# Attention and mixture of experts on one core: a row's expert numbers and shares written by GpSimd, low parts in halves, a new item order

## The reference

```python
x = _layernorm(x + attention(x))      # 16 heads of 16, 4 key/value heads, causal
x = _layernorm(x + ffn(x))
# attention: q, k, v projections, rotation by head number, softmax(q k^T / 4) v, output projection
# ffn:
scores = sigmoid(gate_w x) + gate_b                 # 16 experts
weights, indices = top_k(scores, 4)
weights = weights / weights.sum(-1)
shared = silu(x @ w1_shared) * (x @ w3_shared) @ w2_shared
routed = sum over the 4 experts of weight * (silu((x @ w1[e]) * (x @ w3[e])) @ w2[e])
out = shared + routed
```

## Time and profile before

| | us |
|---|---|
| median of 3 runs | 535.52 (535.23 to 536.46) |
| the profiled execution's own time | 534.25 |
| its span, first to last instruction | 532.5 |
| TensorE busy | 506.3 |
| VectorE busy | 435.0 |
| ScalarE busy | 373.2 |
| GpSimd busy | 292.0 |
| chain that ended last: TensorE, VectorE, ScalarE, GpSimd | 63%, 22%, 6%, 5% |

### The profile page before, as it was taken

One profiled execution on the slowest core, in us unless ns is written; L12 is line 12 of the kernel. 1 busy time (PEld: TensorE's weight loads), 2 busy tenths in 40 slices (PEclk: granted clock), 3 DMA queues, 4 the chain that ended last, 5 costly groups with the idle time before them and its releaser, 6 DMA issues.

```text
span 532.5 us, 12191 instructions
## 1 busy us (share of the span) xinstructions
PE 506.3 (95%) x3775; PEld 359.0 (67%) x3775; DVE 435.0 (82%) x1102; ACT 373.2 (70%) x845; POOL 292.0 (55%) x340
## 2 busy tenths in 40 slices
PE   8789999999999999899999997999999999999895
PEld 5545554545454646355432696899999999999884
DVE  3699998899999999989971479978878877877685
ACT  3527878788988978769889573466766766667444
POOL 5404354454315677777778592777555445445292
PEclk9989999999999999999999999999999999999998
DMA  5464350074034893201422631577543433331595
GB/s 154 94 164 62 78 86 19 3 160 84 1 95 121 182 215 94 82 33 50 130 77 81 183 92 41 181 244 232 154 135 129 121 119 114 117 115 45 192 414 186
DMA packets 53182, 64.96 MB, mean 122 GB/s; under 512 B 8139, under 2 KB 46686, under 8 KB 53120
## 3 DMA queue, kind: packets, MB, share of 16 engines
q1 hardware_dynamic: 45072, 45.60, 32.0%
q0 software_dynamic: 7344, 18.38, 10.1%
q10 hardware_dynamic: 704, 0.20, 0.2%
HBM read 32.49 MB, written 25.62 MB: 109 GB/s over the span
## 4 chain that ended last, share of the span: by engine, by line
PE 63%; DVE 22%; ACT 6%; POOL 5%; issue 3%; DMA 1%; DVEq 0%; ACTq 0%; POOLq 0%
PE psH L1820 15%; DVE MX L1265 10%; PE psO L1602 8%; PE psS L1617 8%; PE psT L1587 7%; PE psX L1788 3%; PE psG L1831 3%; PE psS L1684 2%; ACT prob L953 2%; PE psY L1844 2%; PE psY L1848 2%; PE psY L1845 2%; PE psY L1847 2%; PE psY L1846 2%; PE psS L1622 2%
## 5 line engine op out<-in xcount | busy, mean ns | idle before, releaser
L953 ACT ACTIVATE prob<-psT 128x512 f32<-128x512 f32 (+3 forms) x384 | 166.0, 497 | 34.1 <-PE psT L1587 31.3
L1265 DVE TENSOR_REDUCE MX<-psS 128x1 f32<-128x512 f32 (+3 forms) x304 | 178.9, 652 | 5.0 <-PE psS L1622 2.0
L1617 PE MATMUL psS<-KS,QS 96*128 96x512 bf16 (+3 forms) x384 | 108.0, 330 | 5.2 <-DVE MX L1265 2.8
L906 POOL DMA_INDIRECT y_scratch<-ys,dst x79 | 77.0, 974 | 65.6 <-ACT ys L1115 50.6
L1587 PE MATMUL psT<-QS,KS 98*128 98x512 bf16 (+3 forms) x384 | 107.2, 328 | 0.4
L829 POOL DMA_INDIRECT xs_scratch<-x1row,slotu x64 | 64.8, 1012 | 30.4 <-issue 15.3
L1820 PE MATMUL psH<-wU,xh 128*128 (+1 forms) x380 | 80.9, 334 | 0.5 <-DVE z L1424 0.4
L1602 PE MATMUL psO<-prob,V 128*32 128x512 f32 (+3 forms) x768 | 75.9, 499 | 1.8 <-POOL prob L862 1.7
L862 POOL TENSOR_SCALAR_AFFINE_SELECT prob<-prob 128x512 f32<-128x512 f32 x64 | 42.2, 664 | 58.8 <-ACT prob L953 58.3
L1587 PEld LDWEIGHTS psT<-QS,KS 98*128 98x128 bf16 x384 | 34.5, 97 | 48.5 <-ACT prob L953 21.1
L1820 PEld LDWEIGHTS psH<-wU,xh 128*128 128x128 f32 x380 | 61.8, 189 | 1.2 <-issue 1.1
(11 more groups left out here) (278 smaller groups left out, 1004.0 us busy)
## 6 DMA issues: line engine op xcount, KB each, us to landing
xs<-xs_scratch SPq DMA_DIRECT2D x80, 134.0 KB
y<-y_scratch SPq DMA_DIRECT2D x16, 512.0 KB, 9.7
wU_raw<-in_L_ffn_w_routed_dram SPq DMA_DIRECT2D x32, 176.0 KB, 3.2
QS<-qp SPq DMA_DIRECT2D x42, 128.0 KB, 4.3
xs_scratch<-padrow SPq DMA_DIRECT2D x4, 536.0 KB
xs_scratch<-padrow SPq DMA_DIRECT2D x16, 134.0 KB
x1row<-in_L_attn_x_dram SPq DMA_DIRECT2D x4, 512.0 KB, 6.8
out_dram<-x1row SPq DMA_DIRECT2D x7, 256.0 KB, 2.9
```

Source lines behind the costliest of these rows:

```text
L906: nc.gpsimd.indirect_dma_start(y4_dram, bass.IndirectOffsetOnAxis(ap=dst[:, n % NSEL, t:t + 1], axis=0), ys[:, n % NYS, t, :], None, bound ...
L953: nc.scalar.activation(prob[:, step % NPROB, h, 0:HALF - c0], ps[:, 0:HALF - c0], ACT.Exp).then_inc(s_Tfree, 1)
L1265: found = nc.vector.tensor_reduce(out=MX[:, c0 // HALF, heads[0]:heads[-1] + 1, i - TH * q], in_=src, op=ALU.max, axis=AX_X)
L1617: last = mm(ps[:, e * dist:e * dist + cols], QS[0:ROWS, QAT[(k // 2) % NSLOT], g % 2 * G + h, (i - TH * q) * P:(i - TH * q + 1) * P], KS[b ...
```

## The change

- **Row metadata.** VectorE writes neither ID nor WT any more. `hit` compares with `idx` (unsigned integers) itself; VectorE doubles the sum and takes the reciprocal, and signals `s_share`. GpSimd, at a group's first scatter, waits for `s_slot` (as before) and for `s_share`, then copies the expert numbers into x1row, multiplies `top` by `trec` into x1row, waits for both (`s_field`), and scatters. VectorE's next `route` waits for `s_field`, since it overwrites `idx`, `top` and `trec`.
- **Low parts.** GpSimd's low part of a wU block is two instructions of 128 x 352 in place of one of 128 x 704, in ORDER and after attention. The first block after attention (wU 10) moves from behind the second layer-norm step to behind the first.
- **Warm-up.** GpSimd's first memset writes ones; TensorE waits for that one alone and does 11 products in place of 9.
- **Order.** ORDER is another string with the same number of each letter.

```diff
-WARM = 9
+WARM = 11
 ORDER = """
-aaaaaapdlapappdpldppaaaaaaaaaadaaaaalamapaaplapadxxxaaaxpxxxavxlaxaaxaxxavmaxaadaxdxpxaaxxaxvmvxaxaxaxaxaaexaxxpxvvxaxaa
+aaaaaappadapdpllppdpaaadaaalaaaaaapamaaaaaaalppaxxxaadxpapdaxxalvmxaxaaxaadxxavxaxxaxaxaxxaxvvmxaxaxaxaxaaexxaxvvxxaxaa
...
-asvxacxaxxvxxmcvxxcxvxxnxcxxcxvxxxxxvxnexxrxcvcxxxvxcxxvcxxxcvxxxvxxxonxxxxxvcvvsen
+xvxacaxxxvxxmovcxxxvxxnxxcwxxvxcxncxcrxxcvxexxvxxxvxxcxcvxxxcvxxxvxxxnxxxxxvsvvsen
-LOWS_AFTER = {1: LASTU[0:1], 2: LASTU[1:2], 3: LASTU[2:]}
+LOWS_AFTER = {0: LASTU[0:1], 2: LASTU[1:2], 3: LASTU[2:]}
...
+            for m in (ones_b, tri_b):
+                nc.gpsimd.memset(m[:, :], 1.0).then_inc(s_const, 1)
             for m in (ident, ident_b, mask_b, padrow):
                 nc.gpsimd.memset(m[:, :], 0.0).then_inc(s_const, 1)
-            for m in (tri_b, ones_b):
-                nc.gpsimd.memset(m[:, :], 1.0).then_inc(s_const, 1)
...
                 if n == 0:
+                    tiles = slice(tile_of(b, q * TH), tile_of(b, q * TH) + TH)
                     pool.wait_ge(s_slot, h + 1)
                     pool.wait_ge(s_const, CONSTS)
+                    pool.wait_ge(s_share, h + 1)
+                    nc.gpsimd.tensor_copy(x1row[:, tiles, ID], idx[:, :, 0:TOPK]).then_inc(s_field, 1)
+                    nc.gpsimd.tensor_tensor(x1row[:, tiles, WT], top[:, :, 0:TOPK], trec[:, :, :].to_broadcast([P, TH, TOPK]),
+                                            ALU.mult).then_inc(s_field, 1)
+                    pool.wait_ge(s_field, 2 * h + 2)
...
-                    nc.gpsimd.tensor_tensor(lo, raw, hi.bitcast(F32), ALU.subtract).then_inc(s_wlo2, 1)
+                    for k in range(KC):
+                        nc.gpsimd.tensor_tensor(lo[:, k, :], raw[:, k, :], hi[:, k, :].bitcast(F32), ALU.subtract).then_inc(s_wlo2, 1)
...
-                    idf.unsqueeze(3).to_broadcast([P, TH, TOPK, NE]), ALU.is_equal))
+                    idx[:, :, 0:TOPK].unsqueeze(3).to_broadcast([P, TH, TOPK, NE]), ALU.is_equal))
...
                 link(nc.vector.tensor_reduce(out=tsum[:, :, 0], in_=top[:, :, 0:TOPK], op=ALU.add, axis=AX_X))
-                link(nc.vector.reciprocal(trec[:, :, :], tsum[:, :, :]))
-                nc.vector.scalar_tensor_tensor(out=x1row[:, tiles, WT], in0=top[:, :, 0:TOPK], scalar=0.5,
-                                               in1=trec[:, :, :].to_broadcast([P, TH, TOPK]), op0=ALU.mult, op1=ALU.mult)
+                link(nc.vector.tensor_scalar(tsum[:, :, 0], tsum[:, :, 0], 2.0, None, ALU.mult))
+                nc.vector.reciprocal(trec[:, :, :], tsum[:, :, :]).then_inc(s_share, 1)
...
+                    if h:
+                        dve.wait_ge(s_field, 2 * h)
-                    link(nc.vector.tensor_copy(x1row[:, tiles, ID], idx[:, :, 0:TOPK]))
...
-            pe.wait_ge(s_const, 6)
+            pe.wait_ge(s_const, 1)
```

More of the change, by code:

```diff
@@ L153 @@
 ORDER = """
-aaaaaapdlapappdpldppaaaaaaaaaadaaaaalamapaaplapadxxxaaaxpxxxavxlaxaaxaxxavmaxaadaxdxpxaaxxaxvmvxaxaxaxaxaaexaxxpxvvxaxaa
[L155 to L161, removed]
-asvxacxaxxvxxmcvxxcxvxxnxcxxcxvxxxxxvxnexxrxcvcxxxvxcxxvcxxxcvxxxvxxxonxxxxxvcvvsen
+aaaaaappadapdpllppdpaaadaaalaaaaaapamaaaaaaalppaxxxaadxpapdaxxalvmxaxxaaxaadxxavxaxxaxaxaxxaxvvmxaxaxaxaxaaexxaxvvxxaxaa
+xxaxxaaxvvmxaxaxaeaxxpaxpwxxadvvalaxxxwanxxaxxavvaexaaaxaxxnxsaxvxaaxxaxapvvlmxaxaxnpaavxxaxaexaxaxpaxlapaxxaxdasvvadxax
+xwaaaxxaxaaxnxaxdaxvvxaxxaxaaaxxxpxamdwvvxxaaxawxarxxvvawsrxaaxaxaxxeaxarxaaxasxavvaxaxxwaaxawxaaxsxarraxraxrvvxaxaxaxax
+srxxaxaamvsvxararwaxawxxaxaxxavvxxxeaaanxxaorxxaaxaxvvsrvxxonxaxaxaxalxaaxxwaxarxaxsvmrvvoxaxraxaxawxaxalxaxraxxaxaxrvsv
+maxaxaxaaxxaaexxwaxavovxxraxxwaarxxnaxaxswmvvvxaxxarxxacxaaxxaxvxxxaaxxaxvvexxaxanxaxolaxaxarxcsacxvvmwxaxaxaxarxxvvxacx
+eaxaxxcrxarxsrrxxaxaavmvxxaraxxnxaxsxaaxvvalxcaexaaxxararxxaxaaxvvaxxwaxaxaxxxcacnxvvmarxxaawxxerxxsraaxarrvvaxcxaxaxaxr
+araxxcaxacvrvacsweaccxxarxaxnrxawxnxsaxaxcvvvxrcxawxxarcaarxxrxxarcvmxxaaaxxrxaaxasxxcavrvxxxaarxarxcaxrxaaravvsaxxercxa
+rrcxacaxrcavcxaxaarxaxaxaxrscaxvraxaxrxaacxrvxxxcaaxaxavmcvxxxaaawxxaxvxxxarxxxvvxcexaxacacxacvxxxvcxaxaxacxaccxcaxaxaxa
+xvxacaxxxvxxmovcxxxvxxnxxcwxxvxcxncxcrxxcvxexxxvxxxvxxcxcvxxxcvxxxvxxxnxxxxxvsvvsen
 """
@@ L172 @@
 SPLIT_X = True
+LOW_HALVES = True
+FIELDS_POOL = True
 def weight_units():
@@ L495, in attention_moe @@
         s_slot = sem("s_slot")
+        s_share = sem("s_share")
+        s_field = sem("s_field")
         s_scat = [sem(f"s_scat{i}") for i in range(GROUPS)]
@@ L882, in run @@
                     hi, lo, raw = weight_part(u)
-                    nc.gpsimd.tensor_tensor(lo, raw, hi.bitcast(F32), ALU.subtract).then_inc(s_wlo, 1)
+                    if u[0] == "wU":
+                        for k in range(KC):
+                            last = nc.gpsimd.tensor_tensor(lo[:, k, :], raw[:, k, :], hi[:, k, :].bitcast(F32), ALU.subtract)
+                    else:
+                        last = nc.gpsimd.tensor_tensor(lo, raw, hi.bitcast(F32), ALU.subtract)
+                    last.then_inc(s_wlo, 1)
                 elif kind == "scat":
@@ L1177, in _, with route_hits @@
             nc.vector.memset(nu[:, :], 0.0)
-            def route_hits(tiles):
-                idf = x1row[:, tiles, ID]
+            def route_hits():
                 link(nc.vector.tensor_tensor(
                     hit[:, :, :, :], iota_b[:, :].unsqueeze(1).unsqueeze(1).to_broadcast([P, TH, TOPK, NE]),
-                    idf.unsqueeze(3).to_broadcast([P, TH, TOPK, NE]), ALU.is_equal))
+                    idx[:, :, 0:TOPK].unsqueeze(3).to_broadcast([P, TH, TOPK, NE]), ALU.is_equal))
                 with nc.allow_low_precision("0 or 1 and their sums below 2, exact in bf16"):
@@ L1330, in run @@
                     link(last)
-                    link(nc.vector.tensor_copy(x1row[:, tiles, ID], idx[:, :, 0:TOPK]))
                     if item not in LATE:
-                        route_hits(tiles)
-                        route_shares(tiles)
+                        route_hits()
+                        route_shares()
                 elif kind in ("hits", "shares"):
-                    _, b, q = item
-                    t0 = tile_of(b, q * TH)
-                    (route_hits if kind == "hits" else route_shares)(slice(t0, t0 + TH))
+                    (route_hits if kind == "hits" else route_shares)()
                 elif kind == "counts":
@@ L1802, in up @@
                     pe.wait_ge(s_wlob, len(BORDER))
-                    pe.wait_ge(s_wlo2, len(LASTU))
+                    pe.wait_ge(s_wlo2, KC * len(LASTU))
                     pe.wait_ge(s_Sfree, S_NO[("list", 0)])
```

4 lines of the change are left out of this document (1 added, 3 removed).

## The result

| | before | after |
|---|---|---|
| median of the runs, us | 535.23 (7 runs) | 530.41 (7 runs) |
| ratio, 95% interval | 1 | 0.9926 (0.9905 to 0.9947) |
| ratio of a second measurement (after_again) | 1 | 0.9915 (0.9893 to 0.9937) |
| profiled span, us | 532.51 | 528.60 |

The account below looks back on a forecast made before the run. Bounds: TensorE and VectorE in attention, VectorE from 317.6 to 343.3 us, then TensorE. Terms -1.7 - 0.2 - 0.2 - 0.7 + 0.1 = -2.7 took the median from 535.52 to 532.8 us; range 530.6 to 537.1.

Parts of the forecast that it names:

- signs of being right: VectorE's routing instructions, TensorE's waits behind second routing within 1 us; stretch behind attention about 1 shorter; L1436 within 1.2; steady part unchanged.
- a sign of being wrong: TensorE's select waits over 3 us in total, a new low-clock stretch, or VectorE's comparison as long as a GpSimd low part.
- Part 1, second group: Second routing: less VectorE work ends TensorE's stall of 1.67 us; -1.7 us, ends -2.1 and 0.
- a rival with a chance of 0.11: Without the second routing's stall the clock stays up at 225 to 229 us: another 1.7 less, 531.1 us; chance 0.11.
- Third group: VectorE's share of the third routing: copy removed, gain 0.2 us, ends 0 and 0.2.
- Fourth group: VectorE's share of the routing at 324.7 us: the copy lies on the chain, so 0.2 us gained in full.
- Part 2: GpSimd's two added instructions and wait before a group's first scatter: 0.9 us, offset by one scatter fewer; worth 0.
- GpSimd's queue: Rival: slot-number wait and fields delay the selects behind a group's first scatter, up to 1.3 us per group; 537.1 us, chance 0.17.
- Part 3: Low parts in halves: behind attention VectorE loses 1.0 us instead of 1.75; gain 0.7, ends 1.7 and -0.7.
- Part 4: Warm-up at the start: TensorE begins earlier but does two more products; worth 0, ends -0.9 and +0.1 us.
- Part 5: The new order string: no sign for it, so 0, ends -1.7 and +1.7 us.
- The second cast at the tail: End of attention: a second weight cast, 0.77 us, before ScalarE's last evacuation, which had 0.64 idle; +0.1 us.

Follow-up runs that it names:

- a2_order: The kernel before with only the new order string; ratio 0.9919.
- a1_fields: The kernel before with only the row metadata change: GpSimd writes a row's experts and shares; ratio 0.9929.
- n2_stall: a1_fields with four unused sums on VectorE behind the second routing; ratio 0.9991 to before.
- a4_halves: The kernel before with only the low parts of wU in halves, the first late one an evacuation group earlier; ratio 0.9968.
- n3_swap: The kernel before with two entries of GpSimd's queue exchanged: a scatter goes ahead of the low part at the second routing; ratio 0.9936.
- n1_nudge: The kernel before with three small GpSimd memsets ahead of the low part that met the share product of the second routing; ratio 1.0029.
- d1_moved: The changed kernel with whole low parts behind attention and the second routing's low part moved behind two biases on GpSimd; ratio 0.9985 to before.
- b1_nofields: The changed kernel without the row metadata change: VectorE copies and multiplies again; ratio 0.9936 to before.

## Why the prediction was right, and where not

The direction and the mechanism held: VectorE held up by a low part in the second routing was the largest thing to win. The sizes were off, in both directions, and 1.67 of the 4.39 us of attention were won ahead of that place. Of the signs of being right two did not show: an instruction of the routing took over 1 us (the bias of the scores, 1.65), and the stretch behind attention is 0.30 us longer, not 1 shorter. The others did: TensorE's waits of 0.9 and 0.6 us, L1436 (now L1452) never over 1.00 us, the steady part as long as before. A stretch of lower clock, a sign of being wrong, stands at 24 to 48 us (0.86, where before has 0.93); it cost nothing visible, as a2_order has 1.00 there and the same time to the first evacuation (27.65 against 27.67 us).

**Part 1, second group (forecast -1.7).** The term that was mis-sized. Where the stall goes, the slow stretch goes with it: the fields alone gave 3.17 us, the exchange of two queue entries 2.10. The prediction had this as a rival with a chance of 0.11, because TensorE was half idle from 220 on anyway; a1_fields and n2_stall show that the stall decides. The reason was also too narrow. It was not VectorE's smaller work that counted but that two instructions no longer met, and a later low part had the same effect: it began 0.82 us behind the product's start in a4_halves and 1.22 in n3_swap. The 0.07 of n1_nudge was too little, and in d1_moved the low part met another instruction. In after the fields hardly matter for it: without them the gain in attention is 3.90 of 4.39.

**Third group (-0.2)**: in a1_fields the thirteenth evacuation, ahead of the third routing, comes 2.20 us earlier than in before and the last one 2.18, so 0. **Fourth group (-0.2)**: -0.25 in a1_fields, as forecast: the copy did lie on the chain.

**Part 2 (0)**: right. GpSimd's two instructions took 0.22 and 0.23 us, less than the 0.4 taken, but the scatter behind them waited 0.81 more, so 1.2 in place of 0.9. It was hidden: TensorE's wait for selects is 1.8 us in a1_fields and 0.8 in after, against 1.7, and the rival "GpSimd's queue" stayed away.

**Part 3 (-0.7)**: wrong in sign, +0.54. The step that failed is "With halves each can lose at most one half, 0.94, by chance 0.5 on average". Losses were 0.64 and 0.75, not 0.5, because a VectorE instruction that has just been let go is followed at once by the next one, which meets the start of the next half; and the longer low parts reached a third instruction. The prediction had named this as its other end (a gain of -0.7), with the later instructions as the reason.

The Trainium skill (SBUF — State Buffer, Who interferes with whom) has VectorE blocked for one whole GpSimd instruction. Here it was blocked to the end of a run of them: 1.65 us over two halves in after, 4.64 over most of a bias, the second one and four halves in d1_moved. But behind attention the waits ended with a half (1.17 and 1.00 us), and in before the copy was through at 219.51, after the first of two biases that ran until 220.13. The measurement decides: to cut an instruction shortens the wait only where GpSimd lets go between the pieces, and what makes it let go is not settled. That the doubling is hit at all fits the same section, which counts `tensor_scalar` in a two-port mode among those that contend; whether this one ran in such a mode no trace here shows. Among the instructions that could be hit next the prediction had looked only at those with two inputs.

**Part 4 (0, ends -0.9 and +0.1)**: within its ends. The warm-up started 0.84 us earlier as worked out; what it gives depends on when TensorE's pace rises (below).

**Part 5 (0, ends -1.7 and +1.7)**: -4.41 alone, beyond its end, since the bound took the largest accident as one stall or its slow stretch, 1.7 us each, and not both. Of the 4.41 us 2.57 lie behind the twelfth evacuation, where the long wait and the slow stretch are gone, and 1.84 ahead of it, where the prediction saw nothing to win. The sign could not be had from counting letters. The second cast at the tail (+0.1) cost nothing: from the fifteenth to the last evacuation 12.24 us in both profiles.

**The ending (not foreseen).** 1.1 us are lost behind the last routed tile. In after's chain of waits GpSimd's first sum waits for the gather of the scattered rows:

```profile
489.47 0.97 POOL y_scratch L926
...
490.75 3.87 DMA y_scratch<-ys,dst
...
495.56 5.36 DMA y<-y_scratch
...
501.06 1.30 POOL y L941
```

In before and in a1_fields that sum waits for VectorE's last `w`. The five kernels that have the fields, halves in attention and the new warm-up together have the long ending (30.0 to 30.7). All others have 29.5, among them b1_nofields with halves and warm-up and a1_fields with the fields alone. No kernel has the fields and only one of the other two, so which of those it takes is open. The reason is open too: none of these parts touches code there.

In sum, against -3.91: attention -4.39 (forecast -1.8, without the rival's -1.7), start -1.01 (0), late copy -0.25 (-0.2), late halves +0.54 (-0.7), ending +1.13 (0). The forecast was near because gains and losses that it missed took each other away in part.

## What to carry to other kernels

Before a stall is priced as an engine's load, look how far apart the two colliding instructions start: 0.05 us here, and exchanging two entries of a queue was worth 2 of the 4 us. Gains that end one and the same stall don't add up, so each part has to be run alone and left out, and the stretch is best cut ahead of the stall, since a gain from before it is another one. And a wait of TensorE is to be priced with the clock behind it: here 1.8 us of waiting cost 2.7 (n2_stall) and 1.5 us 2.1 (n3_swap).

## What was not expected of the hardware

**VectorE blocked across GpSimd instructions**, 4.64 us for a doubling of four values, as above.

**TensorE's pace at the start rises at different times in different executions.** From the chains of waits at the start: before, then a1_fields, which has the same code up to there, then a2_order:

```profile
5.92 1.04 PE psS L1648 x4
...
7.16 0.60 PE psS L1673 x4
```

```profile
5.92 1.06 PE psS L1658 x4
...
7.27 1.90 PE psS L1683 x8
```

```profile
9.56 2.05 PE psS L1643 x8
...
11.61 2.51 PE psS L1684 x6
```

The transposes of x took 0.15 us each in before, and 0.24 in a1_fields, where the faster pace came at about 11 us; in a2_order the first six projections still took 2.51 us, which are 1.65 in before. The granted clock in the windows is 1.00 from 0 to 24 us in all three, so only the pace of the instructions shows it. The first row maximum follows: 24.4 to 27.6 us over all kernels, on average 25.4 in the seven profiles with eleven products and 26.2 in the seven with nine. That is the whole of Part 4's gain, if it is one: each group holds a late rise (27.56 and 27.57), and seven profiles each do not settle a difference of 0.8.
